# Layer 1's bias: added to the divided sums by GpSimd, or to the values when VectorE copies h; a two-layer graph transformer on one core

## What is computed

```python
h = einsum('bnd,ade->bane', x1, W)                 # 12 heads of 32
th = tanh(h)
attn = (th . w_src) + (th . w_dst)^T               # leaky relu, mask, softmax over m
feat_out = einsum('banm,bame->bane', attn, h) + b  # b: 32 values, the same for every head
feat_out = elu(feat_out)
gate = sigmoid(x1 @ H_w.T + H_b)
x2 = layernorm(x1 + gate * feat_out + (1 - gate) * x1)
```

## Time and profile before

| what | value |
|---|---|
| median of 3 runs | 1107.05 us (1103.86 to 1107.2) |
| the profiled execution: its own time | 1105.45 us |
| the profiled execution: its span, first to last instruction | 1103.6 us |
| granted TensorE clock, mean | 0.986 |
| busy: PE, DVE, POOL, ACT | 96%, 79%, 64%, 59% |
| DMA | 31.00 MB, mean 28 GB/s |

### The profile page before, as it was taken

One profiled execution on the slowest core, in us unless ns is written; L12 is line 12 of the kernel. 1 busy time (PEld: TensorE's weight loads), 2 busy tenths in 40 slices (PEclk: granted clock), 3 DMA queues, 4 the chain that ended last, 5 costly groups with the idle time before them and its releaser, 6 DMA issues.

```text
span 1103.6 us, 28424 instructions
## 1 busy us (share of the span) xinstructions
PE 1056.6 (96%) x9199; PEld 895.9 (81%) x9199; DVE 872.9 (79%) x2289; ACT 651.4 (59%) x2060; POOL 703.9 (64%) x605
## 2 busy tenths in 40 slices
...
GB/s 188 32 1 33 30 33 15 19 34 21 31 29 31 7 21 31 29 31 20 37 9 21 31 29 31 7 21 31 29 31 29 31 7 21 31 29 2 10 15 36
DMA packets 34722, 31.00 MB, mean 28 GB/s; under 512 B 15872, under 2 KB 34688, under 8 KB 34688
## 3 DMA queue, kind: packets, MB, share of 16 engines
...
## 4 chain that ended last, share of the span: by engine, by line
PE 79%; DVE 12%; issue 6%; ACT 1%; POOL 0%; DMA 0%; DVEq 0%; POOLq 0%; ACTq 0%
PE p_bank L573 50%; PE t_bank L712 5%; PE context L726 5%; DVE weights L1032 4%; PE scores L635 4%; PE context L732 4%; PE t_bank L644 3%; PE context L656 3%; PE t_bank L605 2%; PE t_bank L740 2%; PE t_bank L682 2%; DVE sd L1001 1%; DVE masked L940 1%; DVE neg_max L948 1%; PE t_bank L703 1%
## 5 line engine op out<-in xcount | busy, mean ns | idle before, releaser
L1139 POOL TENSOR_TENSOR w_rows<-qwT,own_head 96x1536 fp32r<-96x1536 f32 x64 | 179.8, 2810 | 87.0 <-ACT qwT L873 87.0
L1032 DVE SCALAR_TENSOR_TENSOR weights<-t_bank,pqw,clip 128x128 f32<-128x128 f32 x768 | 206.4, 344 | 7.4 <-PE t_bank L712 6.6
L1132 POOL TENSOR_TENSOR prod<-th,w_sd 128x768 f32<-128x768 f32 x64 | 118.2, 1846 | 124.8 <-ACT th L836 124.7
L808 ACT ACTIVATE probs<-masked,neg_max 128x128 f32<-128x128 f32 x384 | 148.8, 391 | 46.4 <-DVE neg_max L948 46.4
L573 PE MATMUL p_bank<-xT,w_q 128*128 128x512 f32 x432 | 113.6, 408 | 4.3 <-DVE w_k L917 4.3
L573 PE MATMUL p_bank<-w_v,xT 128*128 128x384 f32 x576 | 115.2, 344 | 1.2 <-DVE clip L985 1.2
L573 PE MATMUL p_bank<-w_f,cT 128*128 128x384 f32 x576 | 115.4, 344 | 0.4 <-DVE cT L910 0.4
L573 PE MATMUL p_bank<-w_h,x1T 128*128 128x384 f32 x576 | 114.0, 343 | 0.2 <-DVE x1T L910 0.2
L573 PE MATMUL p_bank<-w_g,x1T 128*128 128x384 f32 x576 | 113.9, 342 | 0.0
L573 PE MATMUL p_bank<-xT,w_k 128*128 128x512 f32 x432 | 111.5, 402 | 0.0
L1120 POOL TENSOR_TENSOR probs<-probs,rden 128x768 f32<-128x768 f32 x64 | 94.3, 1473 | 25.2 <-DVE rden L953 25.2
...
## 6 DMA issues: line engine op xcount, KB each, us to landing
...
adj_in<-in_adj_dram SPq DMA_DIRECT2D x16, 64.0 KB, 4.3
...
```

What stands on the lines that cost most here:

```text
L808: last = act.activation(probs0[:, k % 2, b, j * P:(j + 1) * P], masked[:, k % 2, b * PAIRS + j, :], ACT.Exp, bias=neg_max[:, b * PAIRS + j ...
L1032: last = dve.scalar_tensor_tensor(out=weights[:, g % 2, n, :], in0=src[:, i * P:(i + 1) * P], scalar=pqw[:, g % 2, 0, n:n + 1], in1=clip[: ...
L1132: pool.tensor_tensor(prod[:], over_heads(th[:], 2), w_sd[:], ALU.mult).then_inc(s_prod, 1)
L1139: pool.tensor_tensor(w_rows[0:QW_ROWS, k % 2], over_heads(qwT[:, k % 2, 1, :].bitcast(F32), H1), per_head(own_head[:], P), ALU.mult).then_ ...
```

## The change

The step `fb` on POOL is taken away, with its buffer f_raw and its semaphore: `f_raw` now writes straight into a buffer of two halves (f_out) that `elu` and `mixa` read. ACT's copy of h is taken away too. In its place DVE has a new step `hb`, which reads h from its PSUM bank, adds b, and writes h to SBUF; it waits for ACT's tanh of the same bank. All twelve tables of the orders are replaced.

```diff
 PE_LOOP = [
-    ("v", 0), ("x1T", 0), ("qk", 0), ("x1T", 1), ("qk", 1), ("qk", 2), ("h", 0), ("gate", 0), ("qk", 3), ("h", 1),
+    ("v", 0), ("x1T", 0), ("x1T", 1), ("qk", 0), ("qk", 1), ("qk", 2), ("h", 0), ("gate", 0), ("qk", 3), ("h", 1),
...
                     act.activation(th[:], src, ACT.Tanh).then_inc(s_th, 1)
-                    wait(act, pe["pv1"], upto(g1, GROUP, k - 1))
-                    act.activation(h[:, k % 2, :], src, ACT.Copy).then_inc(s_h, 1)
...
                     wait(act, s_elu, upto(g1, GROUP, k))
-                    act.wait_ge(s_fb, upto(g1, GROUP, k + 1))
-                    act.activation(f_neg, f_b[:, k % 2, :], ACT.Relu, scale=-1.0,
+                    act.wait_ge(s_fraw, upto(g1, GROUP, k + 1))
+                    act.activation(f_neg, f_out[:, k % 2, :], ACT.Relu, scale=-1.0,
...
+                elif name == "hb":
+
+                    dve.wait_ge(s_th, upto(g1, GROUP, k + 1))
+                    if turn == SECOND and k == 0:
+                        dve.wait_ge(s_bias1, 4 * 16)
+                    wait(dve, pe["pv1"], upto(g1, GROUP, k - 1))
+                    dve.tensor_tensor(h[:, k % 2, :].rearrange("p (h e) -> p h e", h=H1),
+                                      p_bank[p_at("h", k, turn)][:, 0:D].rearrange("p (h e) -> p h e", h=H1),
+                                      over_heads(bias_1[:], H1), ALU.add).then_inc(s_h, 1)
...
-                    wait(dve, s_fb, upto(g1, GROUP, k))
+                    wait(dve, s_mixa, upto(g1, GROUP, k - 1))
                     values = t_bank[t_at("sumsT", k, turn)][:, 0:D].rearrange("p (h e) -> p h e", h=H1)
-                    dve.tensor_tensor(f_raw[:].rearrange("p (h e) -> p h e", h=H1), values,
+                    dve.tensor_tensor(f_out[:, k % 2, :].rearrange("p (h e) -> p h e", h=H1), values,
                                       per_head(rden1[:], HD1), ALU.mult).then_inc(s_fraw, 1)
...
-                    dve.scalar_tensor_tensor(out=mix[:], in0=f_b[:, k % 2, :], scalar=-1.0, in1=exp_less_x,
+                    dve.scalar_tensor_tensor(out=mix[:], in0=f_out[:, k % 2, :], scalar=-1.0, in1=exp_less_x,
...
-                elif name == "fb":
-                    pool.wait_ge(s_fraw, upto(g1, GROUP, k + 1))
-                    wait(pool, s_mixb, upto(g1, GROUP, k - 1))
-                    pool.tensor_tensor(f_b[:, k % 2, :].rearrange("p (h e) -> p h e", h=H1),
-                                       f_raw[:].rearrange("p (h e) -> p h e", h=H1),
-                                       over_heads(bias_1[:], H1), ALU.add).then_inc(s_fb, 1)
```

More of the change, by code:

```diff
@@ L118 @@
+    ("qwTo", 3, 1), ("sumsTo", 2, 1), ("gatet", 2, 1), ("elu", 2, 1), ("sumsTo", 3, 1), ("elu", 3, 1),
+    ("gatet", 3, 1),
 ]
 DVE_LOOP = [
-    ("x1lo", 0), ("gsum", 0), ("x1lo", 1), ("sd", 0), ("sda", 0), ("wlog", 0), ("qwlo", 0), ("sd", 1), ("sda", 1),
-    ("wlog", 1), ("qwlo", 1), ("gsum", 1), ("x1lo", 2), ("mask", 0), ("e", 0), ("max", 0), ("e", 1), ("e", 2),
-    ("mask", 1), ("e", 3), ("e", 4), ("e", 5), ("rden0", 0), ("max", 1), ("rden1", 0), ("x1lo", 3), ("f_raw", 0),
-    ("sd", 2), ("sda", 2), ("rden0", 1), ("wlog", 2), ("gsum", 2), ("mask", 2), ("max", 2), ("sd", 3), ("sda", 3),
@@ L125 @@
-    ("qwlo", 2), ("wlog", 3), ("mixa", 0), ("mixb", 0), ("qwlo", 3), ("sum1", 0), ("rden1", 1), ("clo", 0),
-    ("stats1", 0), ("mask", 3), ("mv1", 0), ("rden0", 2), ("f_raw", 1), ("max", 3), ("e", 6), ("e", 7), ("e", 8),
-    ("sum0", 0), ("stats0", 0), ("clo", 1), ("rden0", 3), ("mv0", 0), ("e", 9), ("e", 10), ("e", 11), ("mixa", 1),
-    ("rden1", 2), ("f_raw", 2), ("mixb", 1), ("sum0", 1), ("clip", 0), ("clo", 2), ("stats0", 1), ("out", 0),
-    ("x1", 0), ("sum1", 1), ("clip", 1), ("mv0", 1), ("stats1", 1), ("sum0", 2), ("mixa", 2), ("rden1", 3),
@@ L130 @@
-    ("mv1", 1), ("f_raw", 3), ("mixb", 2), ("clo", 3), ("stats0", 2), ("xlo", 0), ("sum1", 2), ("mv0", 2),
-    ("gsum", 3), ("xlo", 1), ("x1", 1), ("stats1", 2), ("sum0", 3), ("xlo", 2), ("mv1", 2), ("xlo", 3), ("mixa", 3),
-    ("stats0", 3), ("mixb", 3), ("out", 1), ("mv0", 3), ("sum1", 3), ("stats1", 3), ("mv1", 3), ("out", 2), ("x1", 2),
-    ("x1", 3), ("out", 3),
+    ("x1lo", 0), ("hb", 0), ("x1lo", 1), ("gsum", 0), ("sd", 0), ("sda", 0), ("wlog", 0), ("hb", 1), ("sd", 1),
+    ("sda", 1), ("qwlo", 0), ("wlog", 1), ("qwlo", 1), ("gsum", 1), ("mask", 0), ("x1lo", 2), ("max", 0), ("e", 0),
@@ new lines @@
+    ("e", 1), ("mask", 1), ("e", 2), ("max", 1), ("rden0", 0), ("e", 3), ("x1lo", 3), ("hb", 2), ("e", 4),
+    ("gsum", 2), ("rden0", 1), ("e", 5), ("sd", 2), ("rden1", 0), ("sda", 2), ("wlog", 2), ("f_raw", 0), ("mask", 2),
+    ("hb", 3), ("qwlo", 2), ("sd", 3), ("sda", 3), ("mixa", 0), ("wlog", 3), ("max", 2), ("mask", 3), ("rden1", 1),
+    ("clo", 0), ("f_raw", 1), ("mixb", 0), ("qwlo", 3), ("sum1", 0), ("rden0", 2), ("e", 6), ("max", 3), ("e", 7),
+    ("e", 8), ("stats1", 0), ("mv1", 0), ("rden0", 3), ("sum0", 0), ("e", 9), ("clo", 1), ("stats0", 0), ("e", 10),
@@ L134 @@
+    ("mv0", 0), ("e", 11), ("rden1", 2), ("f_raw", 2), ("mixa", 1), ("x1", 0), ("clo", 2), ("mixb", 1), ("out", 0),
+    ("sum0", 1), ("sum1", 1), ("stats0", 1), ("clip", 0), ("clip", 1), ("mixa", 2), ("stats1", 1), ("sum0", 2),
+    ("mv0", 1), ("mixb", 2), ("xlo", 0), ("xlo", 1), ("clo", 3), ("sum1", 2), ("rden1", 3), ("mv1", 1), ("f_raw", 3),
[3 rows of a table added]
 ]
@@ L142 @@
-    ("clo", 1, -1), ("xlo", 2, -1), ("glo", 1, -1), ("x1", 0, -1), ("xlo", 3, -1), ("sum0", 1, -1), ("clo", 2, -1),
[4 rows of a table removed]
-    ("gsum", 1, 0), ("mask", 0, 0), ("x1lo", 2, 0), ("max", 0, 0), ("e", 3, 0), ("rden1", 0, 0), ("f_raw", 0, 0),
-    ("mask", 1, 0), ("max", 1, 0), ("rden0", 0, 0), ("e", 4, 0), ("e", 5, 0), ("sd", 2, 0), ("sda", 2, 0),
-    ("x1lo", 3, 0), ("wlog", 2, 0), ("rden0", 1, 0), ("mixa", 0, 0), ("mask", 2, 0), ("max", 2, 0), ("mixb", 0, 0),
-    ("qwlo", 2, 0), ("sum1", 0, 0), ("gsum", 2, 0), ("rden1", 1, 0), ("f_raw", 1, 0), ("sd", 3, 0), ("sda", 3, 0),
@@ L151 @@
-    ("rden0", 2, 0), ("wlog", 3, 0), ("mask", 3, 0), ("clo", 0, 0), ("stats1", 0, 0), ("max", 3, 0), ("qwlo", 3, 0),
-    ("e", 6, 0), ("gsum", 3, 0), ("sum0", 0, 0), ("e", 7, 0), ("stats0", 0, 0), ("e", 8, 0), ("mv0", 0, 0),
-    ("rden0", 3, 0), ("mv1", 0, 0), ("mixa", 1, 0), ("clo", 1, 0), ("e", 9, 0), ("mixb", 1, 0), ("clip", 0, 0),
-    ("e", 10, 0), ("rden1", 2, 0), ("f_raw", 2, 0), ("sum1", 1, 0), ("e", 11, 0), ("sum0", 1, 0), ("xlo", 0, 0),
-    ("xlo", 1, 0), ("clo", 2, 0), ("x1", 0, 0), ("stats1", 1, 0), ("stats0", 1, 0), ("mixa", 2, 0), ("out", 0, 0),
[4 rows of a table removed]
@@ L161 @@
+    ("rden0", 1, 0), ("wlog", 2, 0), ("e", 5, 0), ("max", 2, 0), ("qwlo", 2, 0), ("mixa", 0, 0), ("sd", 3, 0),
+    ("sda", 3, 0), ("mixb", 0, 0), ("wlog", 3, 0), ("sum1", 0, 0), ("clo", 0, 0), ("hb", 3, 0), ("rden1", 1, 0),
+    ("f_raw", 1, 0), ("gsum", 3, 0), ("clip", 0, 0), ("qwlo", 3, 0), ("rden0", 2, 0), ("mask", 3, 0), ("e", 6, 0),
[4 rows of a table added]
+    ("rden1", 3, 0), ("mv0", 1, 0), ("xlo", 2, 0), ("f_raw", 3, 0), ("clo", 3, 0), ("clip", 1, 0), ("x1", 1, 0),
[3 rows of a table added]
 ]
 DVE_END = [
-    ("x1lo", 0, 0), ("x1lo", 1, 0), ("gsum", 0, 0), ("sd", 0, 0), ("sda", 0, 0), ("wlog", 0, 0), ("qwlo", 0, 0),
```

142 lines of the change are left out of this document (72 added, 70 removed), and 120 rows, old and new, of tables (DVE_BEGIN, DVE_END, DVE_LOOP, PE_BEGIN).

## The result

The changed kernel takes 1142.26 us (median of 4 runs, 1142.21 to 1142.45), the kernel before on the same chip 1105.45 (1103.56 to 1107.2): a ratio of 1.0335, 95% interval 1.0314 to 1.0356. That is slower by 37 us where I had forecast 1092, and outside the range.

A forecast was written before the change was run, and what follows sets the result against it. PE's list was taken to bound the kernel. A net 0.95 us a turn over 13 turns (12.4 us) plus 1.3 in the drain made 13.7 us off 1105.45: 1092 us, range 1083 to 1106.

The forecast's parts named there:

- The new order, by the waits above: Part on the loop's reordered lists; first item: `rows` of graph 0 starts past `sda`, so its hold goes, 0.33 us a turn.
- 0.5 us for all new waits together: Loop: allowance a turn for the first `wb` close behind `rows`, `qwT` of graph 2 behind ACT's queue, and unhidden weight loads.
- Rival 2: DVE becomes the bound in the turn's crowded stretch: `hb` makes each `e` 0.94 us late, 1116 us; chance 0.14.
- The nine matmuls of 384 columns: PE, between `h` and graph 0's bank being wanted again: estimated 1.6 us, against some 1.2 for tanh, hand-over and `hb`.
- 1.47 less 0.5: Loop's net gain a turn: 1.47 us of waits that go, less 0.5 of new waits, given as 0.95.
- the waits for `rows` and for the copy of k: PE's loop waits: at `rows` 0.27 of 0.37 us goes; `qk`'s 0.2 for the copy of k goes.
- The `wb` behind `pTo`: PE in the loop: the second `wb`'s wait for `pTo` goes, as `pv1`'s matmuls stand between, 0.47 us a turn.
- the wait for `qwlo`: PE in the loop: `qwT`'s wait goes, as `qwT` of graph 0 moves behind both last `qk`, 0.2 us a turn.
- the wait for `pTo` at `pT`: PE in the loop, among the `pT`: claimed to stay, since the new order has the same neighbours there.
- The first `wb`'s 0.33 us: PE's loop wait for the bank freed by the split of x1T, traced to `sda`'s hold; claimed gone, 0.33 us a turn.
- The drain's term: Behind the last `f_raw`: without `fb`, `elu` starts earlier, 1.3 us gained once; bounds 0 and 2.3.
- The ceiling of 2.5 us a turn: All PE waits in a loop turn, the most a better order can give: 2.5 us a turn, 33 us over 13.

The follow-up runs named there:

- e4: The changed kernel with `hb` working on one head's 32 columns instead of 384, the rest of h a constant 1: 1146.9 us, ratio 1.0384 to before.
- e1: The changed kernel with `wlog` written as a TENSOR_REDUCE instead of a TENSOR_SCALAR, same place in DVE's list: 1093.39 us, ratio 0.9907 to before.
- e5: The kernel of e1 with x1 of graph 1 two steps earlier in DVE's loop list: 1087.96 us, ratio 0.9853 to before.
- e11: The kernel before the change, with `sda` and `wlog` written as reductions over pairs, all else as it was: 1099.18 us, ratio 0.9948.

## Why the prediction was wrong

**The step that failed** is "The new order, by the waits above", in its first item. There I read the hold of `sda` rightly from the earlier trace rows, and counted only its removal. The same lists that told me that `sda` leaves the reach of graph 0's `rows` could have told me who enters another's: `wlog` of graph 3 against graph 2's `rows`. I didn't look, for I took the hold to be a matter of two SBUF inputs, as `sda` has, and `wlog` has one. The trace of before speaks against that already, in one row that I had not read: `wlog`'s most there is 2746 ns.

```profile
L1012 DVE TENSOR_SCALAR wlog<-sda x64: 132/174/2746, 64.0 to 1074.5; 128x12 f32<-128x12 f32 x64
```

In the new order the hold of `wlog` lasted 2.55 us in each of the 13 turns and cost 3.9 us a turn, where I had set 0.5 us for all new waits together.

The Trainium skill covers both kinds, in SBUF — State Buffer, section "SBUF: two separate sides": a VectorE instruction in a 2-port mode, or one with two SBUF inputs against a GpSimd instruction that reads SBUF, shuts the other out, for the whole instruction. The runs agree on the length of the hold (2.55 us under a 2.79 us `rows`, 1.27 under a half). That `wlog`'s TENSOR_SCALAR ran in such a mode, no run shows. I had drawn only its second half, and only as a gain.

**The chain behind it was missed too.** I named `hb`, `e`, `rows` and the split of x1T as the steps for which PE might wait. It was `clo`: it frees the context bank, and in the new order nothing but `sumsT` and one projection v (1.83 us) stand between the two `pv0`.

**Rival 2** had the right sign and, as I worded it, the wrong mechanism: DVE's list was late by a hold and not by 0.94 us of work. e4 shows that less work there didn't help.

**What held.**
- `hb`: 554 ns, in the 0.53 to 0.57 that I gave; ACT's and POOL's busy time in a turn, 38.6 and 39.1 us, were near the 38 and 39.5 forecast. The nine matmuls of 384 columns beside it take 1.83 us (the row of v above), where I had estimated 1.6.
- With `wlog`'s hold gone, as in e1, a turn is 0.87 us shorter than before where I had summed 0.95 (1.47 less 0.5 is in fact 0.97), and the time 1093.4 where I had 1092. That closeness is partly luck. x1 is still held in e1; without that hold, as in e5, a turn is 1.39 us shorter. And the composition was worse than the sum. PEld's waits in one turn of e1:

```profile
PEld t_bank L710 <- ACT probs0T L815: 0.5, 1, 0.5
PEld t_bank L680 <- DVE xT L907: 0.4, 1, 0.4
PEld t_bank L642 <- DVE weights L1039: 0.4, 1, 0.4
...
PEld t_bank L701 <- DVE qw_parts L907: 0.2, 1, 0.2
PEld p_bank L571 <- DVE sum L960: 0.2, 1, 0.2
```

Against the earlier trace rows, the waits for `rows` and for the copy of k are gone and `e`'s stays, as I said. The `wb` behind `pTo` still waits, 0.5 us, which I had called gone at 0.47, and the wait for `qwlo` stays at 0.2. On the other side, the wait for `pTo` at `pT` (0.4), which I kept, went. Two waits are new, 0.4 us at `x1T` for the split of xT and 0.2 for `sum0`, 0.6 together where I had set 0.5. The first `wb`'s 0.33 us was no cost of `sda`'s hold: e11 gives 0.06 us a turn.
- The drain's term: from the start of the last `f_raw` to the end of the span it was 12.3 us (1091.34 to 1103.6) and is 10.1 in e1 (1080.79 to 1090.9), 2.2 us less, near my upper bound of 2.3, where I took 1.3. The whole drain is 1.6 us shorter, at a clock of 0.91 against 0.88, so that number says little of the term.
- The ceiling of 2.5 us a turn stands: the shortest turn here is 1.4 us under before's.
